# Graph attention layers on one core: the sj row through a DRAM scratch, redrawn engine orders, four weight staging buffers, and an aggregation on fp32r halves

## The reference

```python
h = max(layernorm0(x), 0)                       # input: 64 x 128 x 256
for l in range(3):
    si, sj = h @ attn_w[l, :256], h @ attn_w[l, 256:]
    s = si[:, :, None] + sj[:, None, :] + attn_b[l]
    s = where(s >= 0, s, 0.2 * s); s = where(mask, s, -inf)
    agg = softmax(s, -1) @ h                    # 128x128 by 128x256 for each graph
    z = layernorm(h + agg) * g1[l] + beta1[l]
    ff = gelu(z @ W1[l] + b1[l]) @ W2[l] + b2[l]    # 256 -> 1024 -> 256
    h = layernorm(z + ff) * g2[l] + beta2[l]
out = x + h
```

## Time and profile before

| quantity | value |
|---|---|
| median of three runs | 1359.9 us |
| profiled execution: time, span of the core | 1360.92 us, 1359.1 us |
| busy: PE, PEld, DVE, ACT, POOL | 93%, 83%, 83%, 68%, 48% |
| granted TensorE clock, mean | 0.987 of full speed |
| chain that ended last: PE, DVE, POOL, issue, DMA | 59%, 26%, 7%, 4%, 2% |
| ACT cast of 128x1024 (L590), mean of one | 1.05 us |
| ACT copy of 128x512 (L634), mean of one | 0.59 us |
| DMA over the span, mean | 29 GB/s |

### The profile page before, as it was taken

One profiled execution on the slowest core, in us unless ns is written; L12 is line 12 of the kernel. 1 busy time (PEld: TensorE's weight loads), 2 busy tenths in 40 slices (PEclk: granted clock), 3 DMA queues, 4 the chain that ended last, 5 costly groups with the idle time before them and its releaser, 6 DMA issues.

```text
span 1359.1 us, 23270 instructions
## 1 busy us (share of the span) xinstructions
PE 1267.5 (93%) x8065; PEld 1133.0 (83%) x8065; DVE 1128.7 (83%) x3325; ACT 924.8 (68%) x1754; POOL 658.0 (48%) x538
## 2 busy tenths in 40 slices
PE   0599999999999999999999999999999999999994
PEld 0388888888888898988888898998888898989983
DVE  4778788889997888889898878879998888888773
ACT  3476766677776677677777776777777677677751
POOL 1235434553565355345545543553565445445454
PEclk9699999999999999999999999999999999999997
DMA  6100001001221000001121100000121100000012
GB/s 205 62 17 17 16 32 40 0 1 41 69 61 50 1 1 1 1 1 32 55 63 32 40 1 1 1 1 3 58 80 41 32 1 1 1 1 1 1 32 78
DMA packets 39265, 39.91 MB, mean 29 GB/s; under 512 B 1736, under 2 KB 37612, under 8 KB 39148
## 3 DMA queue, kind: packets, MB, share of 16 engines
q1 hardware_dynamic: 39148, 38.43, 8.9%
HBM read 30.04 MB, written 8.39 MB: 28 GB/s over the span
## 4 chain that ended last, share of the span: by engine, by line
PE 59%; DVE 26%; POOL 7%; issue 4%; DMA 2%; ACT 1%; SPq 0%; POOLq 0%; DVEq 0%
PE acc L700 28%; PE hbank L685 23%; DVE xs L536 7%; POOL rstd L332 3%; PE util L735 3%; DVE hid_lo L435 3%; PE acc L715 3%; DVE st L454 3%; DVE xs L523 2%; PE util L742 2%; DVE mv L415 2%; DVE st L422 1%; DMA hb<-in_x_dram 1%; DVE st L530 1%; POOL xout L375 1%
## 5 line engine op out<-in xcount | busy, mean ns | idle before, releaser
L700 PE MATMUL acc<-w2hi,hid_hi 128*128 128x256 f32 x1536 | 441.4, 287 | 0.0
L700 PE MATMUL acc<-w2hi,hid_lo 128*128 128x256 f32 x1536 | 434.3, 283 | 0.0
L700 PE MATMUL acc<-w2lo,hid_hi 128*128 128x256 f32 x1536 | 434.1, 283 | 0.0
L332 POOL TENSOR_TENSOR rstd<-ve,halfs 128x4 f32<-128x4 f32 x112 | 122.7, 1095 | 598.2 <-DVE ve L417 598.0
L595 ACT ACTIVATE hbank<-hbank,vec 128x512 f32<-128x512 f32 x384 | 254.6, 663 | 188.2 <-PE hbank L685 184.9
L685 PE MATMUL hbank<-ht_hi,w1hi 128*128 128x512 f32 x768 | 320.2, 417 | 2.5 <-DVE hid_lo L435 2.5
L685 PE MATMUL hbank<-ht_lo,w1hi 128*128 128x512 f32 x768 | 302.6, 394 | 0.0
L685 PE MATMUL hbank<-ht_hi,w1lo 128*128 128x512 f32 x768 | 301.2, 392 | 0.0
L435 DVE TENSOR_TENSOR hid_lo<-hbank,hid_hi 128x512 fp32r<-128x512 f32 x384 | 258.8, 684 | 46.3 <-ACT hid_hi L601 46.3
L700 PEld LDWEIGHTS acc<-w2lo,hid_hi 128*128 128x128 f32 x1536 | 293.7, 191 | 4.0
L700 PEld LDWEIGHTS acc<-w2hi,hid_hi 128*128 128x128 f32 x1536 | 293.3, 191 | 4.0
(11 more groups left out here) (62 smaller groups left out, 1750.1 us busy)
## 6 DMA issues: line engine op xcount, KB each, us to landing
xres<-in_x_dram SPq DMA_DIRECT2D x16, 512.0 KB, 4.0
out_dram<-xout SPq DMA_DIRECT2D x32, 256.0 KB, 2.3
xraw<-in_x_dram SPq DMA_DIRECT2D x14, 512.0 KB, 3.7
xout<-in_L_gnn_W_dram SPq DMA_DIRECT2D x12, 512.0 KB, 3.9
adji<-in_adj_dram SPq DMA_DIRECT2D x16, 256.0 KB, 2.9
hb<-in_x_dram SPq DMA_DIRECT2D x2, 512.0 KB, 9.6
attn_rows<-in_L_gnn_attn_w_dram SPq DMA_DIRECT2D x1, 768.0 KB, 5.7
ln_rows<-in_L_gnn_g_dram SPq DMA_DIRECT2D x2, 384.0 KB, 7.4
```

The lines of the kernel that those rows point to most:

```text
L332: pool.tensor_tensor(rstd[n][:], ve[n][:], halfs[:], ALU.pow).then_inc(rstd_n[n], 1)
L700: mm = pe.matmul(to, v[:, k % HID, of_g], w[:, i.l, c], start=c == 0 and n == 0 and g % HG == 0, stop=c == C - 1 and n == 2, skip_group_ch ...
```

## The change

1. sj no longer passes through PE and `util`: SP writes the dots to a DRAM scratch (2 KB) and reads them back broadcast to all partitions into `sj_bc`; `masked` reads that, four floats apart along j.
2. E and x are split into fp32r halves: ACT writes `ET_hi` and `x_hi`, DVE writes `ET_lo` (`et_low`), POOL writes `x_lo` (`x_low`). `aggregate` is three fp32r matmuls for each graph instead of one fp32 matmul.
3. Four weight halves are fetched at the start into `xout[0]`, `xout[1]`, `xs[2]` and `xres`; the first loads stand in one list.
4. The `slot` functions of all engines have another order and partly another item offset.

```diff
-        ET = sb("ET", [P, GG, P])
+        ET_hi = sb("ET_hi", [P, GG, P], F32R)
+        ET_lo = sb("ET_lo", [P, GG, P], F32R)
+        x_hi = sb("x_hi", [P, GG, D], F32R)
+        x_lo = sb("x_lo", [P, GG, D], F32R)
+        sj_bc = sb("sj_bc", [P, P, GG])
+        sj_dram = nc.dram_tensor("sj_dram", [2, P, GG], F32).ap()
...
+            t = (xout[:, 0], xout[:, 1], xs[:, 2], xres[:])[n if n < 4 else n % 2]
...
+            def send_sj(i):
+                sp.wait_ge(dotj_n, i.q + 1)
+                wait(sp, sj_in, 16 * (i.q - 1))
+                sp.dma_start(sj_dram[i.q % 2], dots[:, 1]).then_inc(sj_sent, 16)
+
+            def load_sj(i):
+                sp.wait_ge(sj_sent, 16 * (i.q + 1))
+                wait(sp, mask_n, i.q)
+                sp.dma_start(sj_bc[:].rearrange("p j g -> p (j g)"),
+                             sj_dram[i.q % 2].rearrange("j g -> (j g)").partition_broadcast(P)).then_inc(sj_in, 16)
...
                 if p and p.l == 0 and s != -4:
                     load_adj(p)
+                if d:
+                    send_sj(d)
+                    load_sj(d)
+            load_xraw(item(0))
+            load_small()
+            load_adj(item(0))
+            load_xraw(item(1))
+            load_b2_rows()
+            load_weights(0)
+            load_weights(1)
+            load_ln1_rows()
+            load_xraw(item(2))
+            load_weights(2)
+            load_weights(3)
+            load_ln2_rows()
...
+            def x_low(i):
+                pool.wait_ge(xhi_n, i.q + 1)
+                pool.tensor_tensor(x_lo[:], x_of(i), x_hi[:].bitcast(F32), ALU.subtract).then_inc(xlo_n, 1)
...
-                t, b, p, o = item(s - 1), item(s + 1), item(s + 4), item(s - 2)
+                t, f, b, a, p = item(s - 1), item(s), item(s + 1), item(s + 2), item(s + 4)
...
+                if a:
+                    x_low(a)
+                if t and t.l == L - 1:
+                    add_input(t, 0)
+                    add_input(t, 1)
+                if f:
+                    make_rstd("2", f.q)
+                if b:
                     h_beta(b, 0)
...
             def masked(i):
                 dve.wait_ge(pen_n, i.g + 1)
-                dve.wait_ge(sj_n, i.q + 1)
                 wait(dve, et_n, i.q)
-                dve.tensor_tensor(sc[:], pen[:, i.g % PENS], util[:].rearrange("p (g j) -> p g j", g=GG),
+                dve.wait_ge(sj_in, 16 * (i.q + 1))
+                dve.tensor_tensor(sc[:], pen[:, i.g % PENS], sj_bc[:].rearrange("p j g -> p g j"),
                                   ALU.min).then_inc(mask_n, 1)
...
+            def et_low(i):
+                dve.wait_ge(ethi_n, i.q + 1)
+                dve.tensor_tensor(ET_lo[:].rearrange("p g j -> p (g j)"), util[:],
+                                  ET_hi[:].rearrange("p g j -> p (g j)").bitcast(F32), ALU.subtract).then_inc(etlo_n, 1)
...
+            def x_high(i):
+                wait_x(act, i)
+                wait(act, agg_n, 2 * i.q)
+                act.copy(x_hi[:], x_of(i)).then_inc(xhi_n, 1)
...
                 for g in range(h * HG, (h + 1) * HG):
-                    mm = pe.matmul(acc_of(i, h)[:, g % HG], ET[:, g], x_of(i)[:, g],
-                                   start=g % HG == 0, stop=True, skip_group_check=True)
+                    for n, (w, v) in enumerate(((ET_hi, x_hi), (ET_hi, x_lo), (ET_lo, x_hi))):
+                        mm = pe.matmul(acc_of(i, h)[:, g % HG], w[:, g], v[:, g],
+                                       start=n == 0 and g % HG == 0, stop=n == 2, skip_group_check=True)
```

More of the change, by code:

```diff
@@ L142, in build @@
         ln2_in = sem("ln2_in")
-        w_in = [sem(f"w_in{i}") for i in range(2)]
+        w_in = [sem(f"w_in{i}") for i in range(4)]
         adj_in = sem("adj_in")
@@ L309, in slot @@
                     load_adj(p)
-            for s in range(-4, ITEMS + 2):
+                if d:
[13 more added lines that the diff above has]
+            load_ln2_rows()
+            for s in range(-6, ITEMS + 3):
                 slot(s)
@@ L396, in slot @@
                     pool.tensor_tensor(ln1_rows[:, 1], ln1_rows[:, 1], b2_rows, ALU.add).then_inc(ln1_ready, 1)
-                if b: h_beta(b, 1)
-            for s in range(-4, ITEMS + 2):
+            for s in range(-6, ITEMS + 3):
                 slot(s)
@@ L464, in j_dots @@
                 wait_x(dve, i)
-                wait(dve, sj_n, i.q)
+                wait(dve, sj_sent, 16 * i.q)
                 if i.q == 0:
@@ L478, in i_dots @@
                 last.then_inc(dots_n, 1)
[L480 to L491, removed]
             def add_bias(i):
@@ L548, in slot @@
                     dve.tensor_copy(vec[:], util[:, 0:NV]).then_inc(vec_ready, 1)
[L549 to L552, removed]
-                if f:
[L554 to L559, removed]
-                if b: norm1(b)
-                if p and p.l == 0: input_moments(p)
@@ L562, in slot @@
-                if f: low(f, 5)
-                if b: h_low(b, 0)
-                if f: low(f, 6)
-                if b: h_low(b, 1)
-                if d: j_dots(d)
-                if f: low(f, 7)
-                split_weights(halves_of_slot(s))
-                if d:
-                    if d.l == 0: penalty(d)
-                    i_dots(d)
-                    add_bias(d)
-                if p and p.l == 0: input_shift(p)
-                if b: low(b, 0)
-                if f:
-                    residual(f, 0)
-                    residual(f, 1)
@@ L578, in slot @@
-                if d: masked(d)
-                if f: moments2(f)
-            for s in range(-4, ITEMS + 1):
+                if a:
+                    moments1(a)
+                if b:
+                    low(b, 3)
+                if d:
+                    masked(d)
+                if f:
+                    norm2(f, 1)
+                if a:
+                    norm1(a)
+                if b:
+                    low(b, 4)
+                if n and n.l == 0:
+                    input_moments(n)
@@ new lines, in slot @@
+                if b:
+                    low(b, 5)
+                if d:
+                    minus_max(d)
+                if b:
+                    low(b, 6)
+                if a:
+                    h_low(a, 0)
+                if b:
+                    low(b, 7)
+                if p:
+                    j_dots(p)
+                    i_dots(p)
+                    add_bias(p)
+                if a:
+                    h_low(a, 1)
+                if n and n.l == 0:
+                    input_shift(n)
@@ new lines, in slot @@
+                split_weights(s + 5)
+                if b:
+                    residual(b, 0)
+                    residual(b, 1)
+                if d:
+                    et_low(d)
+                if b:
+                    moments2(b)
+                if a:
+                    low(a, 0)
+                if p and p.l == 0:
+                    penalty(p)
+                if a:
+                    low(a, 1)
+                if d:
+                    attend(d, 0)
+                if b:
+                    norm2(b, 0)
@@ L582, in _ @@
+                if d:
+                    attend(d, 1)
+                if a:
+                    low(a, 2)
+            for s in range(-6, ITEMS + 3):
                 slot(s)
```

208 lines of the change are left out of this document (105 added, 103 removed).

## The result

The changed kernel takes 1338.1 us (median of 4 runs, 1336.8 to 1339.1), the kernel before 1359.8 us on the same chip (4 runs, 1359.6 to 1360.2). The ratio is 0.984, with a 95% interval from 0.9823 to 0.9857: 22 us faster where I had forecast 50. The profiled execution took 1336.8 us with a span of 1335.0, so the gap between my 1309.7 us of span and what ran is 25.3 us.

A forecast was written before the change was run, and what follows sets the result against it. PE was taken to bound the kernel, DVE's loop of 25.1 us just under PE's floor of 25.35: 58.0 + 34 x 25.45 + 12 x 26.9 + 63.6 = 1309.7 us of span, forecast 1310 us, range 1286 to 1342.

The forecast's parts named there:

- PE's lighter round: PE's floor per round falls from 26.08 to 25.35 us, sj_rows 0.44 and aggregate 0.29; 33.6 us over 46 rounds.
- So the row is just in time: sj row's way through DRAM takes 6.2 us of 6.5 to 7 available in nine rounds; lateness put at 0.
- masked's step of 16 bytes: masked reading the sj row at four fp32 apart: taken at 0.60 us, upper end twice 0.59.
- Rival B: DVE takes over: masked at twice its length or held by POOL, 0.6 us in all 46 rounds, 1338 us; chance 0.24.
- Quiet rounds: The 34 rounds without both loads and stores: PE's floor 25.35 us plus 0.1 for misses, 25.45 us each.
- the chain's sum: DVE's work from an item's last ffn2 to norm1 two items later: 15.2 us, within a loop of 25.1 us.
- norm1: DVE's four norm1 instructions start with POOL quiet, since h_gamma waits for the first half: 2.33 us, bounds 1.46 and 4.13.
- Rounds beside loads: 12 rounds with layer 2 stores and layer 0 loads, delayed by add_input and input_moments: 26.9 us each, up to 29.5.
- The start: Time to item 1's first e_turn: 58.0 us instead of 57.1, bounds 54 and 63.
- Rival A: PE's floor everywhere, every wait behind cover, loads included: 46 rounds of 25.35 us, 1288.5 us; chance 0.20.
- C: POOL's lock: x_low and h_beta run late, so norm1 takes 4.13 us instead of 2.33; 1381 us; chance 0.07.
- D: No effect: row or halves come so late that PE's savings turn into equal waits, 1360 us; chance 0.02.

The follow-up runs named there:

- e8: The changed kernel with sj rows turned by PE and native fp32 aggregate without halves, leaving the new order and four staging buffers: 1318.5 us, 0.9691 of the kernel before.
- e7: The changed kernel with the sj row turned by PE into util as before, no DRAM scratch; order, staging and halves stay: 1308.4 us, 0.9616 of the kernel before.
- after: The changed kernel with all parts of the change, against the kernel before: 1338.1 us, ratio 0.984.
- e2: The changed kernel with the sj row's write and read moved ahead of load_adj in SP's queue: 1310.6 us, 0.9649 of the kernel before.
- e1: The changed kernel with the sj row laid out graph by graph, so masked reads at a step of one, written in 4-byte pieces: 1423.0 us, 1.0474 of the kernel before.
- e5: The changed kernel with the sj row ahead of load_adj and native fp32 aggregate without halves: 1312.7 us, 0.965 of the kernel before.
- e3: The changed kernel with both the graph-by-graph sj row (e1) and the row ahead of load_adj (e2): 1313.0 us, 0.9665 of the kernel before.
- e9: The changed kernel with SP waiting for the sj row to land before issuing anything more: 1322.5 us, 0.9717 of the kernel before.
- e10: e2 with POOL's add_input moved ahead of x_low: 1341.4 us, 0.9859 of the kernel before.

## Why the prediction was right and wrong

**The parts of the change, priced by the runs.** Start from order and buffers alone (e8, 0.9691, some 42 us faster than before). The halves on top of that take 10 us more (e7). The DRAM row on top of that costs 30 us (after, against e7), of which 26 come back when the row goes ahead of load_adj in SP's queue (e2). So the sum of the change is the gain of a new order, less a row that comes late. The forecast had the parts otherwise: 33.6 us from PE's lighter round and 10 from closed gaps. In e8 PE's work is the old one but for 0.13 us a round, and its rounds gain 32 us, 26 of them from closed gaps. The 0.44 us a round that sj_rows had cost on PE, 20 of the 33.6 us, were not gained in sum: no DRAM version is as fast as e7, which still has sj_rows.

**The step that failed is the sj row's**: "So the row is just in time", its lateness "put at 0 in the sum". By e2 it is 26.1 us: 5.8 at the start (62.09 against 56.29), 19.9 in the twelve rounds beside loads (336.8 against 316.9), 0.4 in the rest. Each of its inputs was taken at its best. I had seen that load_adj holds the send until the penalty, and that 6.5 to 7 us are left for a way of 6.2. But the way took 644.54 to 653.08, 8.5 us: the write 2.46, which I had counted at 2.3, and the read 6.06, not 2.9, since four other transfers were issued within 3.7 us behind it. A median of landing times is no price for a transfer that has company, and the trace of before showed the company. Nor did I ask what PE's gap would do to its clock; with that, 2.4 us of wait became 4.9 us of a round (31.29 against e2's 26.4).

**masked's step of 16 bytes** was taken as free (0.60 us, upper end twice). It takes 1.07 us, near that upper end; with a step of one it takes 0.68 (e1). I had 0.25 us of slack in the loop, and 0.39 used it up: quiet rounds are 25.53 and not PE's 25.24, 0.29 us in each. Rival B was this mechanism, but with 0.6 us a round in all 46; its 1338 us, which is the time measured, is a coincidence, since the other 34 rounds exceed the forecast by 7.4 us only. In the first nine rounds the 0.5 us wait and the slack were also to cover split_weights, put at nothing; they didn't, which is 5.4 of the 7.4 us. With masked at 0.67 us (e7) seven of these rounds are no longer than quiet ones. The note of the Trainium skill (SBUF — State Buffer, "Door 1: The DMA port swizzle") says two things, and the runs part them: that each crossing to a new line pays agrees with 1067 against 682 ns, that a step of four fp32 is free doesn't.

**Quiet rounds** were forecast at 25.45 and are 25.53. That is close, with two errors that offset: the floor is 25.24 and not 25.35 (the new order also takes out 0.11 to 0.13 us that was in the old round, e8), and the chain is 25.5 and not 25.1 (the terms of the chain's sum, 15.2 us, add up to 15.3).

**norm1** was right: 649 ns mean, 2.25 to 2.35 us for four, where the earlier trace rows has 4.13. POOL was idle for 1.85 us ahead of h_gamma, which began at 867.59, behind norm1's first half: the reason given. DVE's timeline there:

```profile
866.78 2.35 DVE L562 TENSOR_SCALAR xs<-xs,mv,rstd 128x256 f32<-128x256 f32 x4
```

**Rounds beside loads** without the late row are 26.4 us (e2), against 26.9. The end is 63.45 against 63.6, and the last add no longer waits for x (POOL's timeline; the earlier trace rows has 2.09 us):

```profile
1329.91 2.48 POOL L407 TENSOR_TENSOR xout<-xout,xres 128x512 f32<-128x512 f32 x2
```

**The start** was forecast at 58.0 and is 56.29 with the row in time, 62.09 as it stands, inside its bounds.

So e2 lies at my 1310 us, but by luck: two of its terms, -5.9 us in the loaded rounds and +7.0 in the other 34, offset. Rival A fell with masked, C with norm1, D with the ratio.

**What stays open.** The four staging buffers were never parted from the order, so the 42 us are theirs together. That the halves pay 10 us beside PE's row (e7 against e8) and nothing beside the DRAM row (e2 against e5) fits the quiet rounds; a version with the halves, the row in time, and masked at a step of one without a write in small pieces should keep the 25.24 us a round that e1 and e3 show in their quiet rounds; it was not tried. Of e9's profiled execution the 7.1 us above e2's span are 5.0 at the start and 2.1 in the rounds; its other executions are 4 to 7 us longer, and where they lose that was not settled.

## What to carry to other kernels

Price a transfer by what its queue and the DMA engines are doing when it is issued, not by its median, and put the small transfer that someone waits for ahead of the large ones that nobody does. When work moves off the busiest engine onto a path through memory, compare the microseconds that it frees (0.44 a round here) with what one late arrival costs (up to 5 a round), and keep the version that leaves it where it was as a rival: it won here, by 0.3% over the best DRAM version (0.9616 against 0.9649). Once the bounding engine has a quarter of a microsecond of slack, each edit of 0.3 us on the second engine decides the round.

## What the runs showed of the hardware

- A DVE tensor_tensor of 128x512 with one fp32 operand read at a step of 16 bytes took 1067 ns, at a step of 4 bytes 682 ns, from PSUM 672 ns (e7).
- A 2 KB write to DRAM took 1.4 us in the median as 16 bytes per partition, up to 3.4 in after and 4.0 in e2; in pieces of 4 bytes one took 10.6 us (e1).
- A 256 KB broadcast read landed in 3.9 us when nothing was issued behind it (e9) and in 6.06 us with a load of 512 KB and three transfers more behind it.
- After 3.2 us of idle time PE's granted clock was 0.50 for the next 5 us: six 512-column matmuls took 2.56 us instead of 1.60, 36 of 256 columns 5.28 instead of 4.31. In e10 six took 2.57 us after 2.95 us of idle time (669.43); after another gap of 2.93 us (640.67) the granted clock stayed at 1.00.
- A tensor_scalar on 128x4 numbers took 2.18 us beside one POOL instruction of 2.46 us (0.23 in after, with POOL idle), and dots 0.85 and 1.50 us instead of 0.42 beside add_input (e10).
